# DLRM interaction on one core: ten tables looked up from the first group on, gathered units moved six blocks ahead, groups of eight

## The reference

```python
e = stack([tbl_0[ids[:, 0]], ..., tbl_25[ids[:, 25]]], axis=1)
all_emb = concatenate([bottom_output[:, None, :], e], axis=1)
gram = einsum('bfd,bgd->bfg', all_emb, all_emb)
z = gram[:, triu_i, triu_j]
h = concatenate([z, bottom_output], axis=1)
h = maximum(h @ W_top1 + b_top1, 0)   # 479 -> 512
h = maximum(h @ W_top2 + b_top2, 0)   # 512 -> 256
y = h @ W_top3                        # 256 -> 1
```

## Time and profile before

| | us |
|---|---|
| median of 3 runs | 360.12 (356.73 to 361.67) |
| the profiled execution | 355.85 |
| its span, first to last instruction | 354.1 |
| TensorE matmuls busy | 329.4 (93%) |
| GpSimd busy | 255.7 (72%) |
| VectorE busy | 245.1 (69%) |
| ScalarE busy | 205.0 (58%) |

### The profile page before, as it was taken

The page is one execution under the profiler, slowest core; times in us unless marked ns, Lnnn a source line. Parts: engine busy times, 40 slices in busy tenths (PEclk is TensorE's granted clock), DMA queues, the critical chain, the costliest instruction groups (busy, mean ns, idle before and its releaser), DMA issues.

```text
span 354.1 us, 13649 instructions
## 1 busy us (share of the span) xinstructions
PE 329.4 (93%) x5840; PEld 295.9 (84%) x5840; DVE 245.1 (69%) x720; ACT 205.0 (58%) x349; POOL 255.7 (72%) x274
## 2 busy tenths in 40 slices
PE   0788989999999999999999989999999999999996
PEld 0676979998888989979888889879999798888885
DVE  1999989996676978459763987549885597431412
ACT  3684777522345659549478567565865587572222
POOL 5777777777777777777777777777777777777720
PEclk9999999999999999999999999999999999999999
DMA  6668649422228685576685496584769476532210
GB/s 206 189 173 219 184 127 316 121 55 54 55 54 159 95 165 114 83 155 136 148 115 98 98 175 123 121 99 99 158 125 141 99 130 113 115 83 56 56 31 1
DMA packets 64203, 42.88 MB, mean 121 GB/s; under 512 B 48784, under 2 KB 56464, under 8 KB 64016
## 3 DMA queue, kind: packets, MB, share of 16 engines
q1 hardware_dynamic: 55024, 24.38, 34.8%
q0 software_dynamic: 8448, 17.32, 20.8%
q10 hardware_dynamic: 672, 0.33, 0.3%
HBM read 31.24 MB, written 0.01 MB: 88 GB/s over the span
## 4 chain that ended last, share of the span: by engine, by line
PE 82%; DVE 9%; DMA 3%; ACT 2%; issue 2%; SPq 0%; ACTq 0%; DVEq 0%
PE hot_ps L498 30%; PE gram_ps L476 14%; PE h_ps L530 11%; PE xt_ps L498 9%; PE h_ps L575 8%; DVE onehot L731 5%; PE h_ps L527 4%; PE xt_ps L459 3%; DMA rows_sb<-in_rows_dram 2%; DVE tab L798 2%; PE zt_ps L512 2%; DMA ids_wide<-in_hot_ids_dram 1%; DVE h L788 1%; ACT turned L993 1%; DVE Z L739 1%
## 5 line engine op out<-in xcount | busy, mean ns | idle before, releaser
L445 POOL DMA_INDIRECT X<-in_table_dram,rows_sb x264 | 254.3, 963 | 82.8 <-issue 78.9
L731 DVE TENSOR_SCALAR onehot<-ids_wide,row_value 128x288 fp32r<-128x288 int16 (+2 forms) x575 | 183.9, 390 | 31.6 <-PE hot_ps L498 20.6
L498 PE MATMUL hot_ps<-onehot,tab 128*128 128x288 f32 (+2 forms) x948 | 144.6, 305 | 14.1 <-DVE onehot L731 13.8
L498 PEld LDWEIGHTS hot_ps<-onehot,tab 128*128 128x128 f32 x948 | 132.0, 190 | 17.7 <-issue 15.4
L706 ACT COPY XT<-turned 128x512 int16<-128x512 int16 x82 | 65.7, 885 | 8.7 <-DMA turned<-planes 8.7
L883 ACT COPY XT<-hot_ps 128x288 f32<-128x288 f32 (+2 forms) x66 | 40.1, 658 | 39.8 <-PE hot_ps L498 37.5
L476 PEld LDWEIGHTS gram_ps<-XT 128*27 128x27 f32 x4096 | 45.1, 104 | 20.9 <-issue 15.8
L476 PE MATMUL gram_ps<-XT 128*27 128x26 f32 x4096 | 56.3, 192 | 4.2 <-issue 1.2
L872 ACT COPY planes<-X 128x1024 int16<-128x1024 int16 x41 | 44.3, 1082 | 17.5 <-DMA X<-in_table_dram,rows_sb 17.5
L530 PE MATMUL h_ps<-stage_sb,w_sb 128*128 128x256 f32 (+3 forms) x192 | 44.2, 366 | 0.0
L530 PEld LDWEIGHTS h_ps<-stage_sb,w_sb 128*128 128x128 f32 (+1 forms) x192 | 35.0, 191 | 4.3
(11 more groups left out here) (54 smaller groups left out, 137.8 us busy)
## 6 DMA issues: line engine op xcount, KB each, us to landing
stage_sb<-in_hot_dram SPq DMA_DIRECT2D x20, 256.0 KB, 3.5
X<-in_table_dram,rows_sb POOLq DMA_INDIRECT x264
ids_wide<-in_hot_ids_dram SPq DMA_DIRECT2D x8, 360.0 KB, 5.3
ids_wide<-in_hot_ids_dram SPq DMA_DIRECT2D x4, 400.0 KB, 4.0
bottomT<-in_bottom_t_dram SPq DMA_DIRECT2D x8, 128.0 KB, 3.9
w_sb<-in_w_dram SPq DMA_DIRECT2D x1, 1024.0 KB, 7.0
turned<-planes SPq DMA_TRANSPOSE x41
stage_sb<-in_hot_dram SPq DMA_DIRECT2D x5, 128.0 KB, 2.9
```

The lines of the kernel that those rows point to most:

```text
L445: pool.indirect_dma_start(X[:, n % RING, k, :], None, table, bass.IndirectOffsetOnAxis(idx[:, column:column + 1], 0)).then_inc(gathered[n ...
L498: mm = pe.matmul(hot_bank(i)[:, 0:width(n)], tab[u][:, part, D * c:D * (c + 1)], onehot[p % ONEHOTS][:, c - BITES[u][h], 0:width(n)], star ...
L731: compared = dve.tensor_scalar(onehot[p % ONEHOTS][:, c - BITES[u][h], 0:width(n)], ids_wide[:, k, 0:width(n)], row_value[:, c:c + 1], Non ...
```

## The change

- Group 0 too looks up all ten small tables; the extra units, the late pieces and `SPLIT_STEPS` go. 64 units, 256 gathers. The features' slots in `XT` are reordered accordingly.
- Eight groups of eight blocks; a slice is 22 or 23 lookups of 128x256. The block slots of `XT` go from 17 to 16.
- Units are moved `LEAD` = 6 blocks ahead: the first six in the head (`HEAD_TURNS`), six more by TensorE in blocks 0 to 5, units 12 to 59 by DMA (split in step b for unit b + 6, moved in step b for unit b + 5), the last four by TensorE. The ring `X` holds 8 units.
- TensorE runs `half_tile` for all blocks up to 55, with one call of `gram` for two blocks whose waits stand ahead of the whole run. The third lookup bank is used from group 2 on.
- SyncE: all pieces first, the index rows after five pieces instead of two, and in the loop over b the turn of unit b + 6.
- VectorE in the head: index rows after the first table, one-hots ahead of the split, the memset of `gram_ps` at the end.

```diff
 
-ALWAYS = 16
-SOMETIMES = 4
-HOT = TABLES - ALWAYS
-HOT_BASE = HOT - SOMETIMES
+GATHERED = 16
+HOT = TABLES - GATHERED
 FOUR = 4
 BLOCKS = P // PAD
-TILE_COLUMNS = BLOCKS * (1 + ALWAYS // FOUR)
-BOTTOM_SLOT = ALWAYS + SOMETIMES
+TILE_COLUMNS = BLOCKS * GATHERED // FOUR
+BOTTOM_SLOT = GATHERED
 ROWS = 128
-RING = 4
+RING = 8
 TURNED = 2
-AHEAD = 2
 SHARING = 2
-KEPT = 17
+KEPT = 16
...
-TAKEN = [8, 9, 9, 10, 9, 10, 9]
+TAKEN = [8] * 8
...
+UNITS = BLOCKS * TILES
+LAST = UNITS - 2 * BLOCKS
+THIRD = 2
+FIRST = [HOT * n for n in range(GROUPS + 1)]
+ORDER = [list(range(HOT)) if n < 2 else list(range(HOT))[::-1] for n in range(GROUPS)]
...
-TURN_FROM, TURN_TO = 16, LAST + 1
-BY_DMA = [n for b in range(TURN_FROM, TURN_TO) for n in UNITS_OF[b]]
-DIRECT = [n for n in range(len(UNITS)) if n not in BY_DMA]
+LEAD = 6
+HEAD_TURNS = {2: 0, 4: 1, 5: 2, 6: 3, 8: 4, 9: 5}
+TURN_FROM, TURN_TO = 12, UNITS - BLOCKS
+BY_DMA = list(range(TURN_FROM, TURN_TO))
+DIRECT = [n for n in range(UNITS) if n not in BY_DMA]
...
-            load_piece(1)
+            for q in range(STAGES):
+                load_piece(q)
             sp.dma_start(rows_sb[:, 2 * TILE_COLUMNS:], rows_in[:, 2 * TILE_COLUMNS:]).then_inc(rows_loaded, 16)
-            for q in range(2, STAGES):
-                load_piece(q)
             load_high_ids(0)
-            for q in range(STAGES, FIRST_PIECE[HOT_BASE]):
+            for q in range(STAGES, FIRST_PIECE[HOT]):
                 load_piece(q)
             sp.dma_start(b1_sb[:], b1).then_inc(b1_in, 16)
             load_bottom(0)
             load_low_ids(1)
-            load_late(0)
             load_high_ids(1)
-            for b in range(1, SPLIT_STEPS):
-                load_late(b)
             load_bottom(1)
             load_bottom(2)
             sp.dma_start(w1_sb[:], w1).then_inc(w1_in, 16)
             sp.dma_start(w2_sb[:], w2).then_inc(w2_in, 16)
             sp.dma_start(vec_sb[:], row_vecs.to_broadcast([P, 2, N2])).then_inc(vecs_in, 16)
-            for b in range(2 * BLOCKS, TILES * BLOCKS):
+            for b in range(min(STARTS[1], TURN_FROM - LEAD), LAST):
                 n = GROUP_OF[b]
                 if b == STARTS[n] and n + 1 < GROUPS:
                     load_low_ids(n + 1)
-                turn_units(b)
+                if b + LEAD in BY_DMA:
...
+            def gram(b, count=1):
 
                 t, j = b // BLOCKS, b % BLOCKS
-                if begin == 0:
-                    pe.wait_ge(xt_moved, UNITS_OF[b][-1] + 1)
-                    if b in STARTS:
-                        pe.wait_ge(hot_placed, FIRST[GROUP_OF[b] + 1])
-                    if j == 0:
-                        pe.wait_ge(bottom_placed, t + 1)
-                        wait(pe, z_ready, t)
-                for pos in range(PAD * j + PAD * begin // RUNS, PAD * j + PAD * end // RUNS):
+                n = GROUP_OF[b + count - 1]
+                if b == 0:
+                    pe.wait_ge(pads_zero, 1)
+                pe.wait_ge(xt_moved, b + count)
+                if STARTS[n] in range(b, b + count):
+                    pe.wait_ge(hot_placed, FIRST[n + 1])
+                if j == 0:
+                    pe.wait_ge(bottom_placed, t + 1)
+                    wait(pe, z_ready, t)
+                for pos in range(PAD * j, PAD * (j + count)):
                     group, q = pos // 4, pos % 4
                     at = NG * (group % GROUPS_PER_BANK)
-                    sample = XT[:, b % KEPT, pos % PAD, :]
+                    sample = XT[:, (BLOCKS * t + pos // PAD) % KEPT, pos % PAD, :]
                     mm = pe.matmul(gram_ps[PAD * q:PAD * q + SLOTS, group // GROUPS_PER_BANK, at:at + NG],
                                    sample, sample[:, 1:SLOTS], start=True, stop=True)
-                if end == RUNS:
-                    mm.then_inc(gram_full, 1)
+                mm.then_inc(gram_full, count)
...
-            def step(b):
-                t, j = b // BLOCKS, b % BLOCKS
-                if t >= 2 and (t % 2 == 1 or j > 0):
-                    lookups(*slice_of(b))
-                    gram(b, 0, 1)
-                    mlp(t, j)
-                    gram(b, 1, RUNS)
-                    transposes(UNITS_OF[b + 1])
-                else:
-                    for run in range(RUNS):
-                        lookups(*slice_of(b, run, run + 1))
-                        gram(b, run, run + 1)
-                    transposes(UNITS_OF[b + 1][:-1])
-                    mlp(t, j)
-                    transposes(UNITS_OF[b + 1][-1:])
-
             def half_tile(b):
 
                 t, j = b // BLOCKS, b % BLOCKS
                 lookups(*slice_of(b))
+                if b + LEAD < TURN_FROM:
+                    transposes(b + LEAD)
                 lookups(*slice_of(b + 1))
-                gram(b)
-                gram(b + 1)
+                gram(b, 2)
                 mlp(t, j)
                 mlp(t, j + 1)
+                if b + 1 + LEAD < TURN_FROM:
+                    transposes(b + 1 + LEAD)
 
             def last_blocks():
-                b, t = LAST - 1, TILES - 3
-                lookups(*slice_of(b))
+                b, t = LAST, TILES - 2
                 pe.wait_ge(hot_placed, 1 + max(i for i in range(len(LOOKUPS)) if hot_bank(i) is xt_ps))
-                transposes(UNITS_OF[b + 2])
-                gram(b)
-                mlp(t, BLOCKS - 1)
-                b, t = LAST, TILES - 2
-                gram(b)
+                gram(b, 2)
                 z_transposes(t - 1)
-                gram(b + 1)
-                transposes(UNITS_OF[b + 2])
+                transposes(b + 4)
                 layer1(len(JOBS) - 3, 0)
                 layer1(len(JOBS) - 3, 1)
-                gram(b + 2)
-                transposes(UNITS_OF[b + 3])
+                gram(b + 2, 2)
+                transposes(b + 5)
...
-            for u in range(HOT_BASE):
+            for u in range(HOT):
                 lookups(0, PRODUCTS[0][u], PRODUCTS[0][u + 1])
-                if u == 2:
-                    transposes(UNITS_OF[0][:1])
-                if u == 4:
-                    transposes(UNITS_OF[0][1:])
-            for b in range(TURN_FROM):
-                step(b)
-            for b in range(TURN_FROM, LAST - 2, 2):
+                if u in HEAD_TURNS:
+                    transposes(HEAD_TURNS[u])
+            for b in range(0, LAST, 2):
                 half_tile(b)
-            step(LAST - 2)
             last_blocks()
...
             dve.wait_ge(rows_head_in, 16)
             dve.tensor_tensor(chunks[:, 0:1, :], chunks[:, 0:1, :], starts, ALU.add).then_inc(idx_head_ready, 1)
-            dve.memset(gram_ps[:], 0.0).then_inc(pads_zero, 1)
-            dve.wait_ge(rows_loaded, 16)
-            dve.tensor_tensor(chunks[:, 1:, :], chunks[:, 1:, :], starts.to_broadcast([P, TILES - 1, TILE_COLUMNS]), ALU.add
-                              ).then_inc(idx_ready, 1)
             dve.wait_ge(rows_counted, 1)
             dve.tensor_copy(row_value[:], row_number[:]).then_inc(row_values, 1)
             dve.wait_ge(minus_counted, 1)
             dve.tensor_copy(minus_value[:], minus_number[:]).then_inc(minus_values, 1)
             dve.wait_ge(row_values, 1)
-            for q in range(FIRST_PIECE[HOT_BASE]):
-                split_second(q)
+            for q in range(FIRST_PIECE[HOT]):
+                if q == FIRST_PIECE[1]:
+                    dve.wait_ge(rows_loaded, 16)
+                    dve.tensor_tensor(chunks[:, 1:, :], chunks[:, 1:, :],
+                                      starts.to_broadcast([P, TILES - 1, TILE_COLUMNS]), ALU.add).then_inc(idx_ready, 1)
                 for p in asked_of(q):
                     one_hot(p)
+                split_second(q)
+            dve.memset(gram_ps[:], 0.0).then_inc(pads_zero, 1)
...
                 for i in placed[:1]:
                     place_hot(i)
-                split_words(UNITS_OF.get(b + AHEAD, []))
+                split_words(b + LEAD)
                 for p in pieces_ended(b):
                     one_hot_share(p + ONEHOTS)
                 for i in placed[1:]:
                     place_hot(i)
                 if j == 2:
                     place_bottom(t + 1)
-                for q in LATE_PIECES[PER_STEP * b:PER_STEP * (b + 1)]:
-                    split_first(q)
-                moves(b + 1)
+                if b + LEAD < TURN_FROM:
+                    move(b + LEAD)
+                if b + LEAD - 1 in BY_DMA:
+                    move(b + LEAD - 1)
...
```

More of the change, by code:

```diff
@@ L102, in features @@
 def features(hot, gathered):
-    return [1 + f for f in gathered + hot[HOT_BASE:]] + [0] + [1 + f for f in hot[:HOT_BASE]]
+    return [1 + f for f in gathered] + [0] + [1 + f for f in hot]
 def pair_row(a, b):
@@ L462, in gram, with transposes @@
-            def gram(b, begin=0, end=RUNS):
-                t, j = b // BLOCKS, b % BLOCKS
-                if begin == 0:
-                    pe.wait_ge(xt_moved, UNITS_OF[b][-1] + 1)
-                    if b in STARTS:
```

(16 more changed lines are left out.)

184 lines of the change are left out of this document (62 added, 122 removed).

## The result

| | before | after |
|---|---|---|
| median of the runs | 358.78 (4 runs, 356.73 to 361.67) | 424.07 (4 runs, 419.70 to 430.25) |
| the profiled execution, its span | 355.85, 354.1 | 424.32, 422.6 |

The ratio is 1.1772, with a 95% interval from 1.1628 to 1.1917: slower. The forecast was 408, with 374 to 424 as its range, so the median lies on the rim, 0.07 us past the 424. Its sum stood for a span of 406.6; the span is 422.6.

A forecast was written before the change was run, and what follows sets the result against it. VectorE was taken to bound the head, TensorE the rest, with GpSimd close. Stages 48.5 + 77.5 + 210.1 + 35.0 = 371.1, plus waits 19 + 10 + 6.5 = 406.6, plus 1.75: 408 us, range 374 to 424.

The forecast's parts named there:

- Step 1: Head: all ten small tables split on VectorE before the first gram, 48.5 us against 31.5, +17.0.
- Step 2: Blocks 0 to 15: lookups of 128x256 at 0.127 us, fewer transposes, longer gram runs; 81.9 us becomes 77.5.
- The two meet within the first eight blocks: Early blocks: gathers and TensorE meet, so the lead of six is not fully there; ScalarE's waits short, priced at nothing.
- Step 4: Five group boundaries, b = 16 to 48: ids queued behind a turn delay the second layer2, 3.8 us each, 19.
- The second half of the ids: Late too, behind the turn of unit STARTS[n]+8, but a free stretch of layers follows; put at nothing.
- Step 5: Pair after each boundary: VectorE makes one-hot pair 11 late for the last lookup; 2.0 us, five times: 10.
- Step 6: Boundary b = 8, no layers beside: late ids, then one-hots, end at 19.8 against 13.2; 6.5 us.
- The grams: Blocks in pairs: one run of 128 gram matmuls takes 1.79 us, 14 ns a matmul, for 11 in short strips.
- B: Rival: head only; ids in time or VectorE quick, boundary waits come to 0 to 20; 373 to 393, chance 0.26.
- C: Rival: not slower; gram runs go at 11 ns throughout, no boundary waits; 360.3, chance 0.05.
- D: Rival: faster; GpSimd is the true pace, eight gathers fewer give 10.2 us: 345.7, chance 0.03.
- E: Rival: worse; ids land in 6 to 9 us and one-hots take 0.32 throughout; above 424, chance 0.08.

The follow-up runs named there:

- e1_again: Kernel after, with the low half of the ids asked for four blocks ahead of the boundary (two for b = 8), ahead of the turn: 399.26 us, ratio 1.1141.
- e4_again: Kernel after, with nine matmuls whose product nobody reads ahead of the second layer2 at five boundaries: 415.27 us, ratio to before 1.164.
- e2_again: Kernel after, low ids asked for four blocks early and high ids at the boundary's own block: 652.35 us on a slow chip, before 599.42.

## Why the prediction was nearly right, and where it was short

The stages of the span, from its own sum (steps 4 to 6 put in where they lie: one boundary and b = 8 in the second row, four boundaries and all of step 5 in the third):

| stretch | before | predicted | after |
|---|---|---|---|
| up to the first lookup of block 0 | 31.5 | 48.5 | 45.3 |
| blocks 0 to 15 | 81.9 | 77.5 + 3.8 + 6.5 = 87.8 | 97.9 |
| blocks 16 to 55 | 204.5 | 210.1 + 15.2 + 10 = 235.3 | 243.8 |
| tail | 36.2 | 35.0 | 35.5 |
| sum | 354.1 | 406.6 | 422.6 |

The measurement lies in the range, and the steps that carry the forecast held; that it lies on the rim and not beyond is luck in part. What the sum lacked or had too small (the clock, the late gather, the grams, steps 4 and 6) comes to 26.4 us, and 10.4 of errors the other way stand against it.

- **Step 1** held, 3.2 us too long: +13.8, not +17.0. The index rows were ready at 10.6 us and not 12.6, and VectorE had splits of the next tables to do until then.
- **Step 2's** price of a lookup was right: 45 take 5.56 to 5.68 us, 0.125 each, for 0.127. But the first gram came at 57.4, not near 54. "The two meet within the first eight blocks" was priced at nothing; the last gather of unit 6 had landed only at 52.57, and TensorE stood 4.13 us before it. GpSimd issued that gather at 44.12, and right behind it, at 44.61 and 45.09, SyncE asked for 1.5 MB of weights; from 48 to 52 us the DMA engines were busy in full (share 0.98 and 1.02). In the three runs of the quick chip's session the same gather went out at 41.2 to 41.5, and no such wait came. So it is a close race, not a fixed cost.
- **Step 4** held in its mechanism and its size: 4.42, 4.01, 4.13, 4.24 and 4.97 us at the five boundaries, 21.8 for 19. e1_again takes them away, and its five boundary pairs are 20.7 us shorter; the wait at b = 8 goes with them. **The second half of the ids** was put at nothing because "a free stretch of layers follows"; with the first half early it costs 3.3 us once, at blocks 12 and 13, and a stretch at half clock behind it (102.7 to 109.6).
- **Step 5** held, if seen without step 4 beside it: 2.4 us each in e1_again, for 2.0. In the kernel after the runs of lookups behind the five boundaries are longer by 1.4 each (7.0 in all, for 10), and that length is half clock for the greater part, which gives VectorE time to catch up.
- **Step 6** held: 6.76 us for 6.5.
- **The step that is missing** is what a wait does to the work behind it. The prediction let TensorE go on at 1.00 after each of steps 4 to 6, since the earlier trace rows show nothing else where TensorE never waited over 1.1 us once the grams had begun. Behind the waits of 4 us the second layer2 takes 2.6 to 3.2 us to the next lookup, where it took 1.64 (195.08 to 196.72 in the earlier trace rows): 6.8 us in five. 45 lookups at b = 8 take 8.56 us for 5.68 (2.9), and 23 behind the late gather 4.4 for 3.0 (1.5): 11.2 us, and a part of step 5's 7.0 beside them. In e4_again, which leaves no gap, the five second layer2s take 1.64 us to the next lookup again, and the boundary pairs are 3.8 us shorter.
- **The grams:** 28 runs of 128 took 58.1 us in the trace, from each run's start to the next work, for 28 x 1.79 = 50.1. Their median is 1.8, as predicted; eight take 2.3 to 4.2, with pauses of up to 2.4 us in them.

Summed up, after less predicted: head -3.2, late gather 4.1 + 1.5, step 4 2.8 + 6.8, step 5 -3.0, step 6 0.3 + 2.9, grams 8.0: 20.2, where the spans differ by 16.0. Of the -4.2 left over the lookups are 2.5 (1260 at 0.125 for 0.127); the rest was not followed up.

Of the rivals, **B** (the head alone) fell: without the late ids, e1_again still shows step 5, but at 399 it lies just above B's 373 to 393, so B is about what remains when step 4 is mended. **C** wanted runs of 128 grams below 1.5 us throughout; they do come at 1.2, but only in blocks 52 to 59, when the last gather is out. **D** fell: GpSimd's last gather starts at 358.7, 64 us ahead of the end. **E's** reason (ids landing in 6 to 9 us) did not occur; the time reached its border by another way.

**The rule weighed.** The Trainium skill, "Runtime: NRT & Kernel Launch", section on instruction fetch mechanics, has fetching hidden below the issue pace. In these traces two things make a run of 128 grams longer than 1.2 us, and only one of them looks like fetching.

The first are single pauses of 0.7 to 2.4 us. The DMA packets of the kernel after hold 48 of 16 KB on a queue of kind "instruction", one for every 257 records of TensorE:

```profile
q8 instruction: 48, 0.79, 0.7%
```

The five traces from quick chips have 13 such pauses inside runs of grams, and each of them ends 1.2 to 1.6 us after the end of one of these packets. They come back at the same places of the program: ahead of the last 3 records of the run of blocks 12 and 13 in all four traces of a changed kernel. Here the traces disagree with the rule: fetching is not hidden in a run whose 256 records of TensorE go by in 1.2 us. No run moved the code, so this rests on where and when the pauses fall.

The second is what the gathers do: 1.7 us and more for nearly every run with gather packets beside it on the quick chips, 1.2 without, and some 10.7 for 1.2 on the slow ones. The instruction packets don't explain that: in e2_again they are as many, and as long (median 0.96 us, 0.98 in the kernel after). What of the gathers holds TensorE up, and why so much more on those chips, no run shows.

**Open:** the high ids' and the seventh buffer's share on a quick chip; the time of the kernel after in the quick chip's session; whether the kernel before would suffer from late ids there. None of the runs points to a version that beats the kernel before: the nearest, e1_again, is 11% slower, and its head and blocks 0 to 15 alone (129.5 us up to block 16, for 113.4) hold 16 of its 42 us.

## What to carry to other kernels

A load that stands behind another instruction in a queue inherits that one's wait: when work is moved ahead, go through each queue and ask which other entry now stands behind a later release. Price a stall of the engine that sets the pace with what follows it: here each 4 us of idle TensorE cost 1.0 to 1.6 us more in the next eight matmuls alone, so two rows of the same work, ahead of and behind a stall, belong in the sum. And look at the time of the unchanged kernel in each session before any difference of a few us is read, and compare the stage that the edit touches, not the whole alone: of the filler's 8.8 us only 3.8 lay where it stands.

## What the hardware showed that was not expected

- Waits of TensorE of 4.0 to 6.8 us brought its granted clock to half for 3.4 or 6.8 us, up to 5.2 us of them after it has work again (140.0 to 145.2); behind the waits of 0.5 us in the kernel before it stays at 1.00, and so it does at 184 to 204 us of e4_again, with 18 matmul records laid into the gap. One-hot waits of 1.3 us were followed by 3.4 us at half clock at two of the five boundaries of e4_again, and not at the other three.
- The kernel before took 357 us on one chip and 592 to 601 on three others, at a mean granted clock of 1.00 and of 0.80 to 0.83. In the traces of changed kernels the gram records are of much the same length (median 187 ns in e1_again, 201 in e2_again), and pauses stand between them: 299.4 us of idle time ended by "issue" ahead of the grams in e2_again, for 24.7 in e1_again. The ratio of the variants to the kernel before stayed at 1.07 to 1.13 all the same, which is no sign that the same thing made it. Whether it is the chip or the session can't be told, since each session had one chip.
- A run of 128 grams beside moving gather packets takes some 10.7 us on the slow chips, and 1.2 where none move (210 and 49 runs in nine traces); single pauses of 0.7 to 2.4 us inside such runs end 1.2 to 1.6 us after a 16 KB packet of kind "instruction" (13 of 13 in five traces).
